# Layer 2: GpSimd's indirect stores, gathers and scatters wait for TensorE's progress

## The chip, the cores and the metric

The kernel is one program on 1 core of one Trainium2 chip. The metric is the device time of one execution in microseconds (us), lower is better.

## What is computed

The input is x, 32 sequences of 128 tokens with 128 channels, and a context of the same shape. Two layers follow each other. Each adds gated cross attention (16 heads of 8 channels) and then a gated mixture of 8 experts. Cut to what matters for the change:

```python
x = x + tanh(g_xattn[0]) * attention0(layernorm(x), ctx)
x = x + tanh(g_ffn[0])   * experts0(layernorm(x))      # one expert of 8 a token, 128 -> 256 -> 128
x = x + tanh(g_xattn[1]) * attention1(layernorm(x), ctx)
x = x + tanh(g_ffn[1])   * experts1(layernorm(x))      # two experts of 8 a token, 128 -> 512 -> 128

# experts1: the two best experts of each token, and their normalised weights
probs = softmax(xt @ gate_w.T); top_w, top_i = top_k(probs, 2)
top_w = top_w / (top_w.sum(-1, keepdims=True) + 1e-9)
out = (take(gelu(xt @ w1 + b1) @ w2 + b2, top_i) * top_w).sum(experts)
```

## The kernel before

**Attention.** The 32 sequences are 16 pairs. A layer's attention is a software pipeline: `pair_slots` runs rows p = -4 .. 16 (here "row" means one pass of that loop, some 9 to 12 us), and in each row every engine does its part for pairs at different stages. TensorE's order inside a row is written out by hand in eight units. A unit has `scores_for_maxima` (L954, four matmuls whose maxima VectorE takes in L1435) and one `scores` (L936), which adds 1 to the semaphore `s_banks` and which ScalarE turns into exponentials in L737. L1097 multiplies them with the values. `s_banks` thus counts TensorE's units; in row p, 8 * a.g - 4 + u is its value when u units of the row are done.

**Experts.** `tile_slots` works on tiles: 39 tiles of 128 tokens in layer 1, 39 tiles of 256 token places in layer 2 (a "turn" is one tile's pass here). In turn i of layer 2 TensorE transposes tile i+1 (L915, adds 1 to `xg_t`), does the first product of tile i (L1229, `h_done`) and the second one of tile i-1 (L1251, `y_done`). ScalarE copies the transposed tile (L872), scales the results of tile i-2 (L896, `y_scaled`) and does the gelus (L885). VectorE copies the expert's weights (L1846), works out where the results go (L1853 to L1861, `META_ROW`) and adds the bias to the result of tile i-1 (L1871, into `YS`, eight buffers deep; `y_kept`). Before the second product of tile i-1 TensorE waits for `y_kept` of tile i-2, since both use bank PA.

**GpSimd's indirect DMAs.** GpSimd writes the descriptors of three kinds of transfers in layer 2, and each instruction moves 128 rows picked by an index:

- gathers (L646): the results of layer 1's experts come back for each pair, two a pair, in rows -4 to 2 by the table `GATHERS`. VectorE adds them in L1411.
- stores (L651, `dispatch`): each batch of 128 tokens goes out twice, once to each of its experts' regions in `dispatched`. Groups of pairs are routed as they come (six groups, `GROUPS`). Groups 0 to 3 are stored in the rows p = 7 to 16; there, all stores of a row but the first (`gated`) already wait for a unit each. Groups 4 and 5 follow in `rest_of_stores`, called ahead of the tile loop and in its pass 1; `g_weight` tells that a group is routed.
- scatters (L696): the results of a tile go to their tokens' places in `returned`, two a tile, as soon as ScalarE has scaled them.

SyncE loads a tile's rows (L526) when the groups it may need have landed (`SCAT`, for tiles from 11 on all six groups), when VectorE has the table of tiles (L525), and three tiles ahead of TensorE (`xg_t`). VectorE may write the buffers of tile i again for tile i+8 when scatter i has landed (`await_results`).

Nothing is scheduled by a planner: the order on every engine is that of the code, and the semaphores do the rest.

Of the kernel before, what the change touches and what calls it, by code (L numbers as in the profile page):

```python
# [54 lines left out]
GATHERS = {-4: (2,), -3: (3, 4), -2: (5, 6), -1: (7, 8), 0: (9, 10, 11), 1: (12, 13), 2: (14, 15)}  # L55
# [127 lines left out]
def program(nc, at, x_in, ctx_in, gates_in, wsq_in, wg_in, vec_in, w0_in, w1_in, const_in,  # L183
# [9 lines left out]
    with ExitStack() as ctx:  # L193
# [203 lines left out]

        LOAD_LATER, COMBINE_LATER, STORE_LATER = 7, 6, 11
        COUNTED = (EARLY_GROUP + 2, NEEDED)

        def await_rows(engine, a):

# [159 lines left out]
        def _(pool):  # L562
# [37 lines left out]
            def attention_slot(layer):  # L600
                def slot(p, pair):
                    n, a, z = pair(4), pair(0), pair(-2)
# [4 lines left out]
                    gated = older[1:] if a else []  # L607
# [15 lines left out]
                        nc.gpsimd.tensor_tensor(out=two(n), in0=two(n), in1=BIAS[:, :].unsqueeze(1).broadcast_to([P, 2, D]),  # L623
                                                op=ALU.add).then_inc(x_bias, 1)
                    if layer == 1:
                        for k in GATHERS[p] if p in GATHERS else ():
                            gather_results(Pair(1, k // 4, k % 4))
                    for unit, (k, b) in zip(range(7 - len(gated), 7), gated):
                        pool.wait_ge(s_banks, 8 * a.g - 4 + unit + 1)
                        dispatch(k, b)  # L630
                    if ahead and not a:
                        for k, b in older[2:]:
# [6 lines left out]
                        deviations(z)  # L639
                return slot  # L640

            def gather_results(g):
                if g.p >= 8:
                    pool.wait_ge(combined, g.p - 7)
                for c in range(2):
                    pool.indirect_dma_start(YG[:, g.p % 8, c, :], None, ys[0][:, :],  # L646
                                            bass.IndirectOffsetOnAxis(ap=SLOT[:, 0, g.b + c:g.b + c + 1], axis=0)).then_inc(YGS[g.p % 8], 16)

            def dispatch(k, b):
                d = next(Group(i) for i in range(len(GROUPS)) if Group(i).b <= b < Group(i).b + Group(i).n)  # L650
                pool.indirect_dma_start(xs[:, :], bass.IndirectOffsetOnAxis(ap=SLOT[:, k, b:b + 1], axis=0),  # L651
                                        N[:, b, :], None).then_inc(SCAT[d.k], 16)
# [12 lines left out]
            def rest_of_stores(k, first, end):  # L665

                d = Group(k)
                pool.wait_ge(g_weight, k + 1)
                for i in range(first, end):
                    dispatch(i % 2, d.b + i // 2)  # L670

            def first_experts():
# [13 lines left out]
            def second_experts():  # L686
                rest_of_stores(4, 0, 3)
                deviations(LAST)
                rest_of_stores(4, 3, 12)
                for i in range(TILES[1]):  # L690
                    a = Tile(1, i)
                    if i == 1:
                        rest_of_stores(5, 0, 8)
                    pool.wait_ge(y_scaled, i + 1)
                    for c in range(2):
                        pool.indirect_dma_start(ys[1][:, :], bass.IndirectOffsetOnAxis(ap=META_ROW[:, a.f, c:c + 1], axis=0),  # L696
                                                YS[:, a.f, c, :], None).then_inc(SC[a.f], 16)

            pair_slots(0, attention_slot(0))
            first_experts()  # L700
            pair_slots(1, attention_slot(1))
            second_experts()


# [200 lines left out]
        def _(pe):  # L905
# [223 lines left out]
            def table_counts(part):  # L1129

                n = COUNTED[part]
                pe.wait_ge(totals, part + 1)
# [131 lines left out]
        def _(dve):  # L1264
# [355 lines left out]
            def table_keys(part):  # L1620
# [5 lines left out]
                comparable, valid, minus_k, region, row, limit, key, places, offset = (ONE[:, k:k + 1] for k in range(9))  # L1626
                n = COUNTED[part]
                count = ROWBASE[:, n - 1:n]
# [23 lines left out]
            def table_values(part):  # L1652


                minus_k, region, row, limit = (ONE[:, k:k + 1] for k in (2, 3, 4, 5))
                n = COUNTED[part]
                count = ROWBASE[:, n - 1:n]
# [287 lines left out]
```

## Time and profile before

| | us |
|---|---|
| median of 3 timed runs | 744.86 |
| the three runs | 745.62, 744.86, 735.52 |
| time of the profiled execution | 743.05 |
| its span in the profile | 741.4 |

The span is that of the instructions; the 1.65 us between it and the execution's time lie around it. In the rows below PE is TensorE, DVE is VectorE, ACT is ScalarE, POOL is GpSimd and SP is SyncE; times count from the span's start. Attention of layer 2 runs from about 330 to 547, its experts from there to the end. "Remote" and "another core or an unknown queue" are the profile's names for a wait whose end it can't put down to an instruction; this kernel has one core. "Issue" is time in which an engine waited for nothing that the profile shows. An indirect DMA's row on POOL is the time in which GpSimd writes its descriptors; the data move after it.

### The profile page before, as it was taken

How to read it: one execution, taken by the hardware profiler on the slowest of the kernel's cores; microseconds unless marked ns; L12 is line 12 of the kernel's file. 1: busy time of each engine (PE TensorE's matmuls, PEld its weight loads, DVE VectorE, ACT ScalarE, POOL GpSimd, SP SyncE). 2: the span in 40 equal slices, each digit the busy share in tenths (PEclk: the TensorE clock that was granted, in tenths of full speed). 3: DMA queues.
4: the chain of work that ended last, by engine and by line, in shares of the span. 5: the costliest groups of instructions: out<-in, count | busy, mean ns of one | idle time of the engine just before them, and what ended most of it. 6: DMA issues, size and time to landing. Idle time of an engine off the chain costs nothing.

```text
span 741.4 us, 17439 instructions
## 1 busy us (share of the span) xinstructions
PE 572.9 (77%) x5771; PEld 464.0 (63%) x5771; DVE 486.7 (66%) x1577; ACT 377.5 (51%) x938; POOL 306.3 (41%) x429
## 2 busy tenths in 40 slices
PE   5889999998811057895888988888676639999991
PEld 4667677775610046785656766666465539999991
DVE  5888889986277944434869998888653524336432
ACT  2267677777422023331346766666443526666661
POOL 5412223311100056637543226464656455455543
PEclk9899999999855559998789999999879969999997
DMA  6243444441010013334445545341022112244523
GB/s 187 79 137 114 140 131 127 133 125 37 15 66 1 0 40 87 88 84 113 134 131 156 166 126 170 110 121 54 32 58 79 56 36 80 72 134 150 156 86 108
DMA packets 99863, 72.58 MB, mean 98 GB/s; under 512 B 13272, under 2 KB 93272, under 8 KB 99752
## 3 DMA queue, kind: packets, MB, share of 16 engines
q1 hardware_dynamic: 88496, 53.64, 24.9%
q0 software_dynamic: 6816, 14.10, 6.5%
q10 hardware_dynamic: 4464, 3.73, 1.7%
q8 instruction: 48, 0.79, 0.5%
q14 instruction: 39, 0.32, 0.1%
HBM read 42.14 MB, written 29.85 MB: 97 GB/s over the span
## 4 chain that ended last, share of the span: by engine, by line
PE 53%; DVE 20%; issue 9%; DMA 6%; POOL 3%; another core or an unknown queue 3%; ACT 2%; SPq 2%; POOLq 0%; DVEq 0%; ACTq 0%
PE bank L1229 11%; PE bank L1251 9%; PE bank L915 7%; DVE MX L1435 7%; PE bank L1097 6%; PE bank L954 6%; PE bank L936 4%; PE bank L1243 3%; DMA QS_N<-MH 3%; DVE PT L1753 2%; POOL dispatched L651 2%; PE bank L920 1%; PE bank L1114 1%; DMA KS<-spread 1%
## 5 line engine op out<-in xcount | busy, mean ns | idle before, releaser
L737 ACT ACTIVATE PT<-bank 128x512 f32<-128x512 f32 x256 | 151.6, 600 | 120.0 <-PE bank L936 97.7
L1435 DVE TENSOR_REDUCE MX<-bank 128x4 f32<-128x512 f32 x256 | 171.8, 680 | 41.8 <-PE bank L954 32.7
L954 PE MATMUL bank<-KS,QS_N 96*128 96x128 f16 x1024 | 104.5, 226 | 23.8 <-DVE MX L1435 10.3
L954 PEld LDWEIGHTS bank<-KS,QS_N 96*128 96x128 f16 x1024 | 74.8, 101 | 53.9 <-issue 25.4
L1229 PE MATMUL bank<-XGT,XT_HL_WR 128*128 128x256 f32 (+1 forms) x468 | 101.3, 354 | 8.7 <-ACT XGT L872 7.1
L936 PE MATMUL bank<-QS_N,KS 98*128 98x512 f16 x256 | 100.8, 398 | 6.0 <-DMA QS_N<-MH 4.1
L696 POOL DMA_INDIRECT returned<-PT,META_ROW x78 | 77.2, 990 | 65.9 <-ACT PT L896 49.7
L1251 PE MATMUL bank<-WALL,HT 128*128 x624 | 78.1, 280 | 22.1 <-DVE PT L1871 15.1
L1251 PEld LDWEIGHTS bank<-WALL,HT 128*128 128x128 f32 x624 | 76.7, 195 | 26.1 <-issue 24.2
L1229 PEld LDWEIGHTS bank<-XGT,XT_HL_WR 128*128 128x128 f32 x468 | 78.4, 195 | 18.3 <-ACT XGT L872 9.2
L651 POOL DMA_INDIRECT dispatched<-N,SLOT x64 | 63.6, 994 | 54.0 <-DVE N L1375 30.2
L1097 PE MATMUL bank<-PT,VA 128*32 128x128 f32 x2048 | 74.7, 288 | 3.5 <-ACT PT L737 3.2
L872 ACT ACTIVATE XGT<-bank 128x128 f32<-128x128 f32 (+1 forms) x78 | 25.8, 331 | 93.4 <-PE bank L915 74.4
L679 POOL DMA_INDIRECT PT<-normed,LIST x39 | 38.3, 983 | 79.2 <-DVE LIST L1821 59.5
L1846 DVE COPY XT_HL_WR<-WALL 128x512 f32 (+1 forms) x78 | 35.0, 449 | 51.3 <-PE bank L1243 24.7
L1871 DVE TENSOR_TENSOR PT<-bank,WALL 128x256 f32<-128x256 f32 x39 | 16.6, 425 | 79.3 <-PE bank L1251 52.1
L1097 PEld LDWEIGHTS bank<-PT,VA 128*32 128x32 f32 x2048 | 55.9, 115 | 20.3 <-issue 13.8
L885 ACT ACTIVATE HT<-bank,XT_HL_WR 128x256 f32<-128x256 f32 x156 | 61.6, 470 | 10.0 <-PE bank L1229 5.9
L590 POOL TENSOR_SCALAR MINUS<-MV_N 128x2 f32<-128x2 f32 x31 | 7.3, 234 | 124.7 <-DVE MV_N L1307 124.1
L646 POOL DMA_INDIRECT HT<-returned,SLOT x32 | 31.4, 980 | 18.7 <-DMA returned<-PT 10.1
L920 PE MATMUL bank<-CONST 128*128 128x128 f32 x192 | 33.7, 323 | 0.0
L920 PEld LDWEIGHTS bank<-CONST 128*128 128x128 f32 x192 | 31.2, 233 | 1.6 <-issue 0.6
(245 smaller groups left out, 1013.6 us busy)
## 6 DMA issues: line engine op xcount, KB each, us to landing
spread<-XT_HL_WR SPq DMA_DIRECT2D x96, 128.0 KB
QS_N<-spread SPq DMA_DIRECT2D x128, 48.0 KB
KS<-spread SPq DMA_DIRECT2D x32, 192.0 KB
PT<-dispatched SPq DMA_DIRECT2D x39, 132.0 KB
WALL<-in_w SPq DMA_DIRECT2D x8, 578.0 KB
CT<-in_ctx SPq DMA_DIRECT2D x32, 128.0 KB
returned<-PT SPq DMA_DIRECT2D x39, 64.0 KB
WALL<-in_w ACTq DMA_DIRECT2D x8, 256.0 KB, 2.8
```

The costliest lines, as they stand in the source:

```text
L651: pool.indirect_dma_start(xs[:, :], bass.IndirectOffsetOnAxis(ap=SLOT[:, k, b:b + 1], axis=0), N[:, b, :], None).then_inc(SCAT[d.k], 16)
L696: pool.indirect_dma_start(ys[1][:, :], bass.IndirectOffsetOnAxis(ap=META_ROW[:, a.f, c:c + 1], axis=0), YS[:, a.f, c, :], None).then_inc(S ...
L737: nc.scalar.activation(PT[:, c, 4 * g:4 * g + 4, :].rearrange("p j q -> p (j q)"), ST[i % 2][:, :], ACT.Exp, scale=SCALE[layer]).then_inc( ...
L885: last = nc.scalar.activation(HT[:, a.u, m, :], bank[2 * a.u + m // 2][:, TILE * (m % 2):TILE * (m % 2) + TILE], ACT.Gelu, bias=WR[:, a.t, ...
L915: return nc.tensor.transpose(to, of, ident[0:n, 0:n])
L920: nc.tensor.matmul(to[:, 0:P], ident, ident, start=True, stop=True)
L936: nc.tensor.matmul(ST[i % 2][:, :].rearrange("p (j q) -> p j q", j=J), KS[0:98, x.r, g, c * P:(c + 1) * P], QS[0:98, x.r, J * g:J * g + J, ...
L954: last = nc.tensor.matmul(MB[i % 2][:, j * P:(j + 1) * P], QS[0:96, m.r, J * g + j, c * P:(c + 1) * P], KS[0:96, m.r, g, c * P:(c + 1) * P ...
L1097: last = nc.tensor.matmul(PA[32 * g:32 * g + 32, 256 * c + P * (j // 2):256 * c + P * (j // 2) + P], VA[:, b.r, c, head(g, j), :], PT[:, c ...
L1229: last = nc.tensor.matmul(bank[2 * a.u + m // 2][:, n * (m % 2):n * (m % 2) + n], WR[:, a.t, m * P:(m + 1) * P], XGT[:, a.u, 0:n], start=T ...
L1251: last = nc.tensor.matmul(PA[:, c * D:(c + 1) * D], HT[:, a.u, m, c * P:(c + 1) * P], WALL[:, bass.ds(r + (W1COLS[1] + m * D), D)], start= ...
L1435: V.tensor_reduce(out=MX[:, m.u, 2 * J * g + c:2 * J * (g + 1):2], in_=MB[i % 2][:, :].rearrange("p (j k) -> p j k", j=J), op=ALU.max, axi ...
```

## The change

Nothing is computed differently, and on TensorE, VectorE, ScalarE and SyncE every instruction stays where it was. On GpSimd the order stays too; what is new are waits ahead of some of the indirect DMAs, in layer 2 alone:

- gathers of rows 0, 1 and 2 (14 instructions; in rows below 0 there is no wait): the first of a row waits for 1 unit of the row, the second for 2, and so on up to 6.
- the stores that already waited for a unit in a row now spread over units 2 to 7, where they waited for the last ones (four of them: units 4, 5, 6, 7 before, 2, 3, 5, 7 now; six rows have such stores).
- the stores of groups 4 and 5: by `STORE_BEHIND`, store 5 of group 4 waits for the transposes of tile 3, store 8 for tile 4, store 11 for tile 5; store 2 of group 5 for tile 7 and store 6 for tile 8.
- the scatters of tiles 1 to 15 wait for the transposes of a later tile as well: tile 8 for scatter 1, 9 for 2, 10 for 3 and 4, 11 for 5, 12 for 6 and 7, 13 for 8, 14 for 9 and 10, 15 for 11, 16 for 12 and 13, 17 for 14, 18 for 15.

```diff
+        STORE_BEHIND = {(4, 5): 3, (4, 8): 4, (4, 11): 5, (5, 2): 7, (5, 6): 8}
...
-                        for k in GATHERS[p] if p in GATHERS else ():
-                            gather_results(Pair(1, k // 4, k % 4))
-                    for unit, (k, b) in zip(range(7 - len(gated), 7), gated):
-                        pool.wait_ge(s_banks, 8 * a.g - 4 + unit + 1)
+                        for i, k in enumerate(GATHERS[p] if p in GATHERS else ()):
+                            gather_results(Pair(1, k // 4, k % 4), 8 * a.g - 4 + 2 * i + 1 if a else None)
+                    for i, (k, b) in enumerate(gated):
+                        pool.wait_ge(s_banks, 8 * a.g - 4 + 2 + 5 * i // max(len(gated) - 1, 1))
                         dispatch(k, b)
...
-            def gather_results(g):
+            def gather_results(g, unit=None):
                 if g.p >= 8:
                     pool.wait_ge(combined, g.p - 7)
                 for c in range(2):
+                    if unit and unit + c > 0:
+                        pool.wait_ge(s_banks, unit + c)
...
                 for i in range(first, end):
+                    if (k, i) in STORE_BEHIND:
+                        pool.wait_ge(xg_t, Tile(1, STORE_BEHIND[k, i]).g + 1)
                     dispatch(i % 2, d.b + i // 2)
...
                     pool.wait_ge(y_scaled, i + 1)
+                    if i in range(1, 16):
+                        pool.wait_ge(xg_t, Tile(1, i + 7 - (i - 1) // 3).g + 1)
```

The order on GpSimd in the first passes of layer 2's tile loop, from scatter 0 on. Before (`dispatched` are the stores of group 5, `returned1` the scatters; in brackets the semaphores that an instruction waits for, and x7 says that the row stands seven times):

```order
L696 DMA returned1<-PT,META_ROW 18176x128
L651 DMA dispatched<-N,SLOT 34816x132 [waits g_weight]
L651 DMA dispatched<-N,SLOT 34816x132 x7
L696 DMA returned1<-PT,META_ROW 18176x128 [waits y_scaled]
L696 DMA returned1<-PT,META_ROW 18176x128
```

And now, with the changed kernel's line numbers, the same place:

```order
L703 DMA returned1<-PT,META_ROW 18176x128
L654 DMA dispatched<-N,SLOT 34816x132 [waits g_weight]
L654 DMA dispatched<-N,SLOT 34816x132
L654 DMA dispatched<-N,SLOT 34816x132 [waits xg_t]
L654 DMA dispatched<-N,SLOT 34816x132 x3
L654 DMA dispatched<-N,SLOT 34816x132 [waits xg_t]
L654 DMA dispatched<-N,SLOT 34816x132
L703 DMA returned1<-PT,META_ROW 18176x128 [waits xg_t,y_scaled]
L703 DMA returned1<-PT,META_ROW 18176x128
```

Nothing moved; the eight stores, which had one wait in front, are cut into 2, 4 and 2, and the scatter behind them has a wait for TensorE too.

The gathers of layer 2's row 0 on GpSimd (`HT` holds the gathered rows), before:

```order
L617 TENSOR_TENSOR RSTD<-VE,EXPO 128x2 [waits pool_own]
L646 DMA HT<-returned,SLOT 128x128 [waits combined]
L646 DMA HT<-returned,SLOT 128x128
L646 DMA HT<-returned,SLOT 128x128 [waits combined]
L646 DMA HT<-returned,SLOT 128x128
L646 DMA HT<-returned,SLOT 128x128 [waits combined]
L646 DMA HT<-returned,SLOT 128x128
```

And now:

```order
L618 TENSOR_TENSOR RSTD<-VE,EXPO 128x2 [waits pool_own]
L649 DMA HT<-returned,SLOT 128x128 [waits s_banks,combined]
L649 DMA HT<-returned,SLOT 128x128 [waits s_banks]
L649 DMA HT<-returned,SLOT 128x128 [waits s_banks,combined]
L649 DMA HT<-returned,SLOT 128x128 [waits s_banks]
L649 DMA HT<-returned,SLOT 128x128 [waits s_banks,combined]
L649 DMA HT<-returned,SLOT 128x128 [waits s_banks]
```

Each of the six has a wait of its own for TensorE's units now; the order is the same.

## Rows read from the trace of the kernel before

**Rows 1.** Line L651: what ended GpSimd's idle time before it, us, times

```profile
  PE bank L936: 9.4, 8
```

**Rows 2.** The chain that ended last, in order of time: start us, us, what

```profile
370.76 2.29 another core or an unknown queue
...
379.50 2.07 another core or an unknown queue
...
588.93 14.94 another core or an unknown queue
...
614.07 1.78 PE bank L1251 x16
...
617.80 1.78 PE bank L1251 x16
...
730.70 2.22 DMA returned<-PT,META_ROW
```

**Rows 3.** Timeline of GpSimd, 557 to 620: start us, us, instruction [idle before <-releaser]

```profile
557.91 1.09 POOL L651 DMA_INDIRECT dispatched<-N,SLOT  x1 [0.17 <-issue]
...
563.33 0.96 POOL L651 DMA_INDIRECT dispatched<-N,SLOT  x1 [0.30 <-issue]
...
570.96 0.95 POOL L696 DMA_INDIRECT returned<-PT,META_ROW  x1 [0.30 <-issue]
581.30 0.96 POOL L651 DMA_INDIRECT dispatched<-N,SLOT  x1 [9.39 <-DVE N L1375]
...
600.28 0.96 POOL L696 DMA_INDIRECT returned<-PT,META_ROW  x1 [0.30 <-issue]
605.43 0.95 POOL L696 DMA_INDIRECT returned<-PT,META_ROW  x1 [4.19 <-ACT PT L896]
...
617.68 0.96 POOL L696 DMA_INDIRECT returned<-PT,META_ROW  x1 [1.05 <-ACT PT L896]
```

**Rows 4.** Timeline of TensorE, 563 to 605

```profile
568.68 2.05 PE L1251 MATMUL bank<-WALL,HT 128*128 x16 [3.35 <-issue]
...
584.56 1.95 PE L1251 MATMUL bank<-WALL,HT 128*128 x16
...
587.49 0.38 PE L915 MATMUL bank<-CONST,PT 128*128 128x128 f32 x2
...
604.67 3.60 PE L1251 MATMUL bank<-WALL,HT 128*128 x16 [15.08 <-DVE PT L1871]
```

**Rows 5.** Timeline of VectorE, 561 to 604

```profile
568.01 0.42 DVE L1871 TENSOR_TENSOR PT<-bank,WALL 128x256 f32<-128x256 f32 x1 [6.40 <-remote]
...
574.02 0.42 DVE L1871 TENSOR_TENSOR PT<-bank,WALL 128x256 f32<-128x256 f32 x1 [4.07 <-remote]
...
604.00 0.42 DVE L1871 TENSOR_TENSOR PT<-bank,WALL 128x256 f32<-128x256 f32 x1 [14.89 <-remote]
```

**Rows 6.** Timeline of ScalarE, the same stretch

```profile
603.97 0.38 ACT L872 ACTIVATE XGT<-bank 128x256 f32<-128x256 f32 x1 [13.30 <-remote]
```

**Rows 7.** DMA queues from 589 to 604: packets, MB, share of 16 engines

```profile
q0 software_dynamic: 352, 0.73, 14.5%
q1 hardware_dynamic: 144, 0.14, 3.6%
```

**Rows 8.** Timeline of GpSimd, gathers of layer 2's rows 0 and 1

```profile
364.51 1.07 POOL L646 DMA_INDIRECT HT<-returned,SLOT  x1 [0.19 <-issue]
...
370.91 0.95 POOL L646 DMA_INDIRECT HT<-returned,SLOT  x1 [0.30 <-issue]
...
375.75 1.08 POOL L646 DMA_INDIRECT HT<-returned,SLOT  x1 [0.18 <-issue]
...
379.63 0.94 POOL L646 DMA_INDIRECT HT<-returned,SLOT  x1 [0.30 <-issue]
```

**Rows 9.** Timeline of ScalarE behind these gathers

```profile
373.11 0.60 ACT L737 ACTIVATE PT<-bank 128x512 f32<-128x512 f32 x1 [2.81 <-remote]
...
381.63 0.60 ACT L737 ACTIVATE PT<-bank 128x512 f32<-128x512 f32 x1 [3.52 <-remote]
```

## The prediction, made before the changed kernel ran

> **What bounds the kernel now.** I read the chain that ended last first. In layer 2's experts it is TensorE alone: from one second product to the next it takes 3.73 us (617.80 - 614.07, [rows 2]), the turns of the last 33 tiles run like that, and GpSimd isn't on that chain until its last scatter. But ahead of these turns the chain has a piece of 14.94 us that belongs to nothing ("another core or an unknown queue", at 588.93), and two more in attention, 2.29 and 2.07 us (370.76 and 379.50, [rows 2]). The question is what these are, since the change touches only GpSimd's indirect DMAs.
>
> The timelines of the four engines answer it. TensorE ran the second product of a tile at 584.56 and the transposes of tile 8 at 587.49 [rows 4]. VectorE needs only the first for its addition L1871, ScalarE only the second for its copy L872. Yet VectorE starts at 604.00 after 14.89 us of idleness, ScalarE at 603.97 after 13.30 [rows 5, 6], within 0.03 us of each other, and TensorE, which needs VectorE's addition, at 604.67 after 15.08 [rows 4]. So TensorE had done the work, but the others didn't learn of it: its semaphore counts were held back. What GpSimd does in that time is a run of 16 indirect DMAs from 581.30 to 601.24 (600.28 + 0.96), 0.3 us apart, eight stores and the scatters of tiles 1 to 4 [rows 3]. The hold ends 2.7 us behind the last.
>
> The same picture stands at every long run. The stores of group 4 and scatter 0 are 11 in a row from 557.91 to 571.9 (570.96 + 0.95, [rows 3]); VectorE waits 6.40 and 4.07 us for "remote" [rows 5], the second time until 2.1 us behind the run, and TensorE is idle for 3.35 us before 568.68 [rows 4]. The six gathers from 364.51 end at 371.86, and ScalarE goes on at 373.11 (1.25 us later); the four from 375.75 end at 380.57, and it goes on at 381.63 (1.06 later) [rows 8, 9]. Where GpSimd pauses after two, as with the scatters from 605.43 on (a wait of 1.05 us ahead of 617.68, [rows 3]), the turns keep 3.73 us. My reading: a run of indirect DMAs can hold back TensorE's counts, mostly until 1 to 2.7 us after the run stops (568.01 came in the middle of one, so not always). What makes it is not in the trace; that they coincide is.
>
> **The change part by part.** Its new waits are on TensorE's counts. While these are held, GpSimd stops at the next wait, and stopping is what ends the hold. The waits thus bound the hold; where no hold exists they are nearly met on arrival, since GpSimd is behind TensorE there. I take 1.25 us as the time from the end of a run to the release.
>
> *Stores of group 4 and scatter 0.* Stores 3 to 11 and two scatters ran in one piece. Now store 8 waits for tile 4. The one ahead of it starts at 563.33 and ends at 564.3 [rows 3]; the release comes at about 565.5, not 568.01: 2.5 us. The second hold (4.07 us) is cut by the wait ahead of store 11, by about 1.6, as three more DMAs still follow that wait. Sum -4.1. Bounds: 0, if holds begin anew at once, and -7.4, TensorE's 3.35 and VectorE's 4.07 us gone.
>
> *Stores of group 5 and scatters 1 to 4.* The idle 15.08 us of TensorE is what is at stake [rows 4]. The run of 16 becomes 2, 4, 4 (two stores and scatter 1) and then twos. The first four take 4 x 1.26 = 5.0 us (spacing from [rows 3]: (600.28 - 581.30) / 15 = 1.26) and with the release 6.3; TensorE can go on for about one turn, 3.73, before it lacks VectorE's addition, so up to 3.2 us remain of that hold allowing 0.6 for the addition and its wait, and 2.2 of the next, which finds GpSimd partly through. 15.1 - 5.4 = 9.7 us gained. Bounds: 0 and -15.1.
>
> *Scatters that share a wait.* 3 with 4, 6 with 7, 9 with 10, 12 with 13: four in a row, 5.0 + 1.25 - 3.73 - 1.4 (the scatters start behind the transposes) = 1.1 us each if each is held; I take half of four: +2.2, bounds 0 and +4.4. All these scatters ran on time before, from 605.43 on.
>
> *Gathers.* In row 1 the second gather waits for unit 2, so the hold of 375.75 to 381.63 should end sooner; in row 0 the first four waits count layer 1's units and are met, only the sixth can stop. 1 us for row 0, 1.5 for row 1, of the 2.29 and 2.07 on the chain [rows 2]: -2.5, bounds 0 and -4.4. The results aren't late: gather 11 of row 0 is added in row 1, behind five of its units.
>
> *Gated stores of groups 0 to 3.* They move by a unit or two to the front, but most find their unit done: TensorE ended only 9.4 us of GpSimd's idle time ahead of the 64 stores, in eight waits [rows 1]. The last one still waits for unit 7. I take 0, bounds -1 and +1.
>
> *What stands behind the waits.* Behind a waiting store are the other stores; tile 11's load needs them all. But it also needs the table that VectorE writes in turn 8, later than store 7 of group 5 (which goes in turn 7), so it hides 2.5 us of stores; without that cover TensorE would wait for the load. Behind scatter 1 stands the reuse of its buffers by tile 9 in VectorE's turn 8. Counted from tile 8's transposes: two stores and two scatters 5.0 us, landing 1.3 (the last scatter of all is issued at 730.70, written by 731.65 and on the chain for 2.22 us, [rows 2]), 6.3 in all; TensorE lacks the result only after 2 turns plus some 1.4 us, 8.9. Slack 2.6 us, so 0.
>
> Sum: 743.05 - 4.1 - 9.7 + 2.2 - 2.5 + 0 = 728.95 us on the profiled execution's own time. The median of the runs lies 1.81 above it, so 730.8; I say **730**.
>
> **Rivals.** *(a) The holds vanish.* Short runs aren't held at all, as in the last 33 turns: 743.05 - 7.4 - 15.1 - 4.4 = 716.2, with the 1.8 us to the median 718, and up to 721 with what stays of row 0. For it: pairs are clean [rows 3]. Against: four gathers in a row were held [rows 8, 9].
>
> *(b) The run is not the cause.* Then the 15 us come back wherever, and the time is 743 to 745. The engines all stand still together, as they would if they lacked instructions. The DMA queues from 589 to 604 show only GpSimd's and the hardware's own packets, and none of the instruction kind [rows 7], which speaks against it; so does that both engines resume as the run ends. In the Trainium skill, page "Runtime: NRT & Kernel Launch", section "Instruction fetch mechanics", instructions are fetched in blocks by DMA of the sequencer's own, and a block that isn't there stalls the engine; by that, waits on GpSimd would change nothing. No packet in [rows 7] agrees. Likewise "SBUF — State Buffer", section "Who interferes with whom", says that a DMA never contends with a compute engine; by that the run couldn't hold TensorE up and the sum would be 743. The trace has 14.89 us of VectorE waiting beside it [rows 5], so I weigh it little.
>
> *(c) Slower.* A hold begins at every new piece. The waits from store 5 of group 4 to scatter 12 name 13 different tiles; at each, both sides stop in turn: GpSimd waits for a held count, and the count waits for GpSimd to be still. At 2.7 us each, the longest release seen, that is 35.1 us against the 15.1 + 7.4 recovered: 743.05 + 12.6 = 755.7, 757 at the median. It decides from 1.7 us a wait on. For it: the release of 568.01 was followed by a second hold within 3 us [rows 5]. Against: the last 33 turns have a pair each and no such stop.
>
> *(d) The waits do little*, since holds last whatever GpSimd does (568.01 ended in mid-run, so some end by another clock): half of the gain, 743.05 - 7 + 1.8 = 738.
>
> **How the numbers follow.** Forecast (724 to 735) 0.51; (a) 0.17; (d) 0.13; (b) 0.12; (c) 0.07. The timed runs of before themselves spread by 10 us, more than any fixed part of the work explains, which fits holds of changing length. The range 719 to 744 leaves out (c), half of (b) and the tip of (a), some 0.17 in all. Two per cent, about what a measurement of this kernel can tell from no change, is 14.9 us: 729.96 is the border, and the forecast lies on it. Faster by over 2%: (a) 0.17 and half of the forecast's case, 0.43. Slower by over 2% needs 759.8, a bad (c): 0.04. Within 2%: the rest, 0.53.
>
> **What would show it.** In the profile after, no piece of over 6 us without an owner between 575 and 605; VectorE's idle time before L1871 put down to "remote" falls from 6.40 + 4.07 + 14.89 = 25.4 us to below 12; GpSimd's stores 2 and 6 of group 5 and scatters 1 to 4 start behind waits that TensorE ended; the turns stay at 3.73 us. Wrong would be: a hold of ten or more us with GpSimd standing still (then (b)); many holds of 1 to 3 us, one for each wait (c); VectorE waiting for a scatter's landing before L1853 or L1855, or SyncE's load of tile 11 ending a wait of TensorE.

## The result, and the profile after

| | before | after |
|---|---|---|
| median of 20 timed runs, us | 743.40 | 737.27 |
| their range, us | 735.52 to 746.95 | 731.59 to 740.75 |
| profiled execution: time, span, us | 743.05, 741.4 | 732.34, 730.7 |

The ratio is 0.9928, 95% interval 0.9905 to 0.9952: faster by 0.7%, some 6 us, and less than two per cent. The time lies inside the range of the prediction, but the gain is less than half of the 14.9 us that stood there (744.86 - 730). The profiled execution flatters the change: it is 10.7 us shorter than that of before, and 7.7 us of this lie ahead of layer 2's first gather (it starts at 323.6 us, before at 331.3), where both programs are the same. This part varies from execution to execution (323.8 to 330.4 us in the other kernels of this study), so below I compare the parts behind it.

In the changed kernel the lines are 7 further down: the second product is L1258, VectorE's addition L1878, the copy of a transposed tile L879, the gelus L892, the scatters L703, the stores L654. The chain of waits, in order of time (start us, us, what), answers to [rows 2]:

```profile
362.42 1.27 another core or an unknown queue
...
370.63 2.16 another core or an unknown queue
...
557.31 3.77 another core or an unknown queue
...
563.17 2.59 another core or an unknown queue
...
593.74 4.38 another core or an unknown queue
...
598.94 2.77 PE bank L1258 x16
...
604.45 2.48 another core or an unknown queue
607.91 3.41 another core or an unknown queue
...
662.28 1.78 PE bank L1258 x16
```

The piece of 14.94 us is gone. In its place stand pieces of up to 4.4 us, among them those of 593.74, 604.45 and 607.91, where the chain of before had TensorE's turns of 3.73 us and nothing else. In attention both pieces are still there, 8 to 9 us earlier, as all of layer 2 is: 2.29 us behind the gathers of row 0 became 1.27, and 2.07 us behind those of row 1 became 2.16. GpSimd's timeline (start us, us, instruction, idle before it and what ended it), 573 to 622, answers to [rows 3]:

```profile
573.44 0.96 POOL L654 DMA_INDIRECT dispatched<-N,SLOT  x1 [3.89 <-DVE N L1382]
...
575.97 0.96 POOL L654 DMA_INDIRECT dispatched<-N,SLOT  x1 [0.30 <-issue]
...
582.64 0.95 POOL L654 DMA_INDIRECT dispatched<-N,SLOT  x1 [1.93 <-remote]
...
589.25 0.95 POOL L703 DMA_INDIRECT returned<-PT,META_ROW  x1 [1.67 <-remote]
...
595.59 0.96 POOL L703 DMA_INDIRECT returned<-PT,META_ROW  x1 [0.30 <-issue]
598.91 0.96 POOL L703 DMA_INDIRECT returned<-PT,META_ROW  x1 [2.36 <-remote]
...
602.63 0.96 POOL L703 DMA_INDIRECT returned<-PT,META_ROW  x1 [1.50 <-PE bank L922]
...
609.05 0.96 POOL L703 DMA_INDIRECT returned<-PT,META_ROW  x1 [0.30 <-issue]
612.34 0.96 POOL L703 DMA_INDIRECT returned<-PT,META_ROW  x1 [2.34 <-remote]
```

The run of 16 is cut, but not into 2, 4, 4 and twos. At 575.97 store 2 found its wait met and went on (0.30 us, "issue"), and so did scatter 1 at 585.16, so the pieces are 6, 4, 6, 2, 6 and 6 DMAs. The six from 589.25 to 596.55 (595.59 + 0.96) are scatters 2, 3 and 4: when the first was let through, tile 10's count came in while it and the next were being written. Each piece of six ends in a wait of GpSimd's own of 1.9 to 2.4 us for a count that TensorE had passed: a small hold. VectorE's timeline in that stretch, to be read beside [rows 5]:

```profile
591.93 0.42 DVE L1878 TENSOR_TENSOR PT<-bank,WALL 128x256 f32<-128x256 f32 x1
...
598.26 0.42 DVE L1878 TENSOR_TENSOR PT<-bank,WALL 128x256 f32<-128x256 f32 x1 [4.39 <-remote]
```

And TensorE's, beside [rows 4]:

```profile
592.61 2.05 PE L1258 MATMUL bank<-WALL,HT 128*128 x16 [0.78 <-DVE PT L1878]
...
598.94 2.05 PE L1258 MATMUL bank<-WALL,HT 128*128 x16 [2.33 <-DVE PT L1878]
...
602.77 1.95 PE L1258 MATMUL bank<-WALL,HT 128*128 x16
```

VectorE waits 4.39 us for "remote" until 598.26, 1.7 us behind the run of six, and TensorE's next second product comes 6.33 us after the last (598.94 - 592.61), not 3.73. Summed over the kernel, VectorE's waits of this kind fell little (the view of waits; us in total, times, longest):

```profile
DVE PT L1878 <- remote: 21.5, 7, 4.4
```

Before, it was 25.4 us in 3 waits; I had said below 12.

**A measure for all kernels.** The start of a second product less that of the one before it, less 3.73 us, is what a turn costs beyond TensorE's own work: its extra time. 39 tiles make 38 gaps. In us:

| gaps | before | after |
|---|---|---|
| 1 to 4 (stores of group 4, scatter 0) | 1.8, 3.9, 3.0, 1.5 | 1.5, 1.3, 1.0, 1.8 |
| 5 to 8 (stores of group 5, scatter 1) | 0.1, 16.4, 1.8, 0 | 0.1, 3.4, 1.0, 1.0 |
| 9 to 16 | 0, all | 2.6, 0.1, 0, 2.9, 0.6, 1.6, 0.1, 1.4 |
| sum of 1 to 8 | 28.5 | 11.1 |
| sum of 9 to 36 | 0.0 | 10.5 |

The change takes 17.4 us out of the first eight turns and puts 10.5 back into the later ones.

Gap 7 of before, 1.8 us, is the hold's as well. The views of windows of both kernels (stretch, its length, busy us of TensorE, its weight loads, VectorE, ScalarE and GpSimd, then the granted clock as a share of full speed), first before, then after:

```profile
604.00:608.50 4.50, 3.83 (x22) 3.82 (x23) 2.88 (x18) 2.49 (x7) 2.16 (x2) 0.56 0.06 21
575.00:604.00 29.00, 22.35 (x152) 19.61 (x151) 14.98 (x78) 14.11 (x41) 17.27 (x19) 1.00 0.24 70
```

After its 15.08 us of idleness TensorE starts again at the lower of its two clock levels (0.50, which is 1.2 GHz, from 604 to 606), and the second product takes 3.60 us [rows 4] where it takes 1.95 at 1.00. In the changed kernel no wait of TensorE there is over 2.33 us, and the granted clock stays at 1.00 from 557 to 714. So a long hold costs more than its idle time, which the prediction didn't count.

So the questions for the chip were: which part does what, what causes the holds, and why do the later turns cost 10 us.

### The profile page after: what moved, and what is told of

The parts are those of the page before. It is cut to its first block, busy times and chain, and to the rows that moved or that the text cites. A ratio compares the mean times of both kernels' runs of the same rounds, so it can differ in the third digit from the quotient of the medians.

```text
span 730.7 us, 17461 instructions
## 1 busy us (share of the span) xinstructions
PE 570.3 (78%) x5771; PEld 458.1 (63%) x5771; DVE 489.4 (67%) x1577; ACT 377.3 (52%) x938; POOL 306.7 (42%) x429
## 3 DMA queue, kind: packets, MB, share of 16 engines
q10 hardware_dynamic: 4464, 3.73, 1.8%
## 4 chain that ended last, share of the span: by engine, by line
PE 52%; DVE 23%; issue 10%; DMA 4%; ACT 3%; another core or an unknown queue 3%; SPq 1%; POOL 1%; DVEq 1%; POOLq 0%; ACTq 0%
PE bank L1236 9%; PE bank L922 7%; PE bank L1258 7%; DVE MX L1442 7%; PE bank L1104 6%; PE bank L961 6%; PE bank L943 5%; PE bank L1250 3%; DVE PT L1760 2%; DMA QS_N<-MH 2%; PE bank L1022 1%; PE bank L1121 1%; PE bank L1024 1%; PE bank L927 1%
## 5 line engine op out<-in xcount | busy, mean ns | idle before, releaser
L703 POOL DMA_INDIRECT returned<-PT,META_ROW x78 | 77.3, 990 | 61.5 <-ACT PT L903 32.3
L1236 PEld LDWEIGHTS bank<-XGT,XT_HL_WR 128*128 128x128 f32 x468 | 79.3, 198 | 14.9 <-ACT XGT L879 6.9
L1258 PE MATMUL bank<-WALL,HT 128*128 x624 | 78.0, 278 | 12.9 <-ACT HT L892 4.7
L1258 PEld LDWEIGHTS bank<-WALL,HT 128*128 128x128 f32 x624 | 74.1, 192 | 21.6 <-issue 20.6
L654 POOL DMA_INDIRECT dispatched<-N,SLOT x64 | 63.5, 993 | 52.1 <-DVE N L1382 23.4
L892 ACT ACTIVATE HT<-bank,XT_HL_WR 128x256 f32<-128x256 f32 x156 | 61.6, 473 | 20.7 <-remote 11.6
L879 ACT ACTIVATE XGT<-bank 128x128 f32<-128x128 f32 (+1 forms) x78 | 25.8, 331 | 73.6 <-PE bank L922 55.9
L1878 DVE TENSOR_TENSOR PT<-bank,WALL 128x256 f32<-128x256 f32 x39 | 16.6, 425 | 68.1 <-PE bank L1258 45.9
L649 POOL DMA_INDIRECT HT<-returned,SLOT x32 | 31.5, 984 | 18.8 <-DMA returned<-PT 10.2
L1250 PE MATMUL bank<-XT_HL_WR,HT 128*128 128x128 f32 x156 | 26.6, 296 | 6.9 <-issue 5.0
L903 ACT ACTIVATE PT<-PT,META_W 128x128 f32<-128x128 f32 x78 | 27.1, 398 | 9.3 <-DVE PT L1878 6.7
```

The costliest lines, as they stand in the source:

```text
L892: last = nc.scalar.activation(HT[:, a.u, m, :], bank[2 * a.u + m // 2][:, TILE * (m % 2):TILE * (m % 2) + TILE], ACT.Gelu, bias=WR[:, a.t, ...
L1236: last = nc.tensor.matmul(bank[2 * a.u + m // 2][:, n * (m % 2):n * (m % 2) + n], WR[:, a.t, m * P:(m + 1) * P], XGT[:, a.u, 0:n], start=T ...
L1250: last = nc.tensor.matmul(bank[6 + a.u][:, 0:D], HT[:, a.u, m, 0:P], WR[:, a.t, w:w + D], start=(m == 0), stop=(m == M - 1))
L1258: last = nc.tensor.matmul(PA[:, c * D:(c + 1) * D], HT[:, a.u, m, c * P:(c + 1) * P], WALL[:, bass.ds(r + (W1COLS[1] + m * D), D)], start= ...
```

## The experiments

Each kernel was timed in five rounds, four at a time beside the same runs of the kernel before; the ratio is to before. First the parts alone.

**Stores alone (e1).** The waits of the scatters and of the rows are taken out again:

```diff
-                    if i in range(1, 16):
-                        pool.wait_ge(xg_t, Tile(1, i + 7 - (i - 1) // 3).g + 1)
```

> The change's waits of the stores of groups 4 and 5 alone; gathers, gated stores and scatters as before. Theory (a run of indirect DMAs without a pause holds TensorE's counts until it stops): the run of 11 is cut as in the changed kernel, 4 to 5 us gained there; the run of 16 begins two stores later and goes on through the scatters of tiles 1 to 6 without a wait, so a hold of some 8 to 12 us stays. About 737 to 741, ratio 0.990 to 0.997. Rival (the waits of the stores are all that counts, since the runs of scatters do no harm): as the changed kernel or better, 0.985 to 0.993.

**Scatters alone (e2).** Only the two lines that e1 takes out are added to the kernel before.

> The change's waits of the scatters of tiles 1 to 15 alone. Theory: the eight stores of group 5 and scatter 1 are still ten in a row, so a hold of 7 to 10 us instead of 15 stays, and behind it GpSimd catches up with holds of 1 to 3 us, 8 to 12 us in all. 741 to 746, ratio 0.997 to 1.003. Rival (the scatters' waits do the work): 0.990 to 0.995.

**Rows alone (e3).** Only the gathers' waits and the spread of the gated stores are added to the kernel before.

> The change's waits in the rows of attention alone (gathers of rows 0 to 2, gated stores spread). The prediction's term: 2.5 us gained, 741, ratio 0.9966. The two profiles differ by 3.9 us up to the first expert product, which would be 0.995. Rival: the difference of the two profiles is chance, and the ratio is 0.999 to 1.001.

**The change with a slower catch-up (e5).** A scatter falls back on its own tile by one tile in six:

```diff
-                    if i in range(1, 16):
-                        pool.wait_ge(xg_t, Tile(1, i + 7 - (i - 1) // 3).g + 1)
+                    if i in range(1, 34):
+                        pool.wait_ge(xg_t, Tile(1, i + 7 - (i - 1) // 6).g + 1)
```

> The whole change, but scatter i waits for tile i+7-(i-1)//6 instead of i+7-(i-1)//3, for tiles 1 to 33: GpSimd catches up by one tile in six turns, not in three. Theory (the loss behind turn 7, 12 us in the changed kernel's profile, is that of runs of four to six scatters while GpSimd catches up): pairs with a pause behind them are clean as in the last turns before, and one four in six turns costs 1 to 2 us, 3 to 6 in all; 728 to 732, ratio 0.980 to 0.986. Rival 1 (each scatter costs what it costs): as the changed kernel, 0.992. Rival 2 (scatters so late make VectorE wait for the buffers of a tile eight later): 0.995 to 1.01, with VectorE's idle time before L1853 or L1855 in the profile.

| | median us | ratio (95%) | extra, gaps 1 to 8 | 9 to 36 |
|---|---|---|---|---|
| e1 stores | 736.11 | 0.9903 (0.9868 to 0.9938) | 22.0 | 3.1 |
| e2 scatters | 739.04 | 0.9948 (0.9921 to 0.9975) | 18.9 | 10.1 |
| e3 rows | 744.98 | 1.005 (1.0015 to 1.0085) | 30.8 | 0.7 |
| e5 slow catch-up | 735.40 | 0.9884 (0.9845 to 0.9922) | 11.3 | 13.4 |

With the stores' waits alone the long hold moves to where the next long run begins, 14 DMAs from 583.81 to 601.62, and gaps 5 to 9 cost 19.0 us together, where before has 18.3. TensorE's timeline of e1:

```profile
588.99 2.05 PE L1256 MATMUL bank<-WALL,HT 128*128 x16 [0.60 <-issue]
...
604.77 3.78 PE L1256 MATMUL bank<-WALL,HT 128*128 x16 [10.38 <-DVE PT L1876]
```

It loses 12.0 (604.77 - 588.99 - 3.73) and 2.6 us in gaps 8 and 9 (the product of 3.78 us behind the hold is again one at a granted clock of 0.50), and the turns behind them are clean, as before. Timed, that gives as much as the whole change, so what the scatters' waits add to the stores' can't be told from nothing by the times: e1 has 0.9868 to 0.9938, f1 below, which has both and no waits in the rows, 0.984 to 0.9925. The scatters' waits alone leave gap 6 at 5.5 us and cost 10.1 later. The rows' waits make the kernel slower by 0.5%, and the slow catch-up spreads its extra time over gaps 13 to 27 without making it less (13.4 against 10.5), so e5 misses its expectation of 0.980 to 0.986.

**Without the rows' waits (f1), gathers alone (f2), gated stores alone (f3).** f1 is the change less what e3 has; f2 and f3 are the halves of e3.

> The change without its waits in the rows of attention: the waits of the stores of groups 4 and 5 and of the scatters. Theory (the parts add up: the rows' waits alone measured 1.005, and they cost the whole change that much): 0.9928 less 0.005 is 0.988, about 733 to 735. Rival (the rows' waits only looked slow, or only cost when the later holds are there too): as the whole change, 0.992 to 0.994.

> Of the change only the gathers' waits for units in rows 0 to 2. The prediction had 2.5 us of gain for it, 0.9966. In the profiles of the change and of the rows alone these waits hardly end any idle time of GpSimd, so they should be without effect: 0.999 to 1.001. Rival (they are what costs in the rows): 1.003 to 1.006.

> Of the change only the spread of the gated stores over units 2 to 7. Theory (spreading them forward joins them to the store or chain ahead and splits the row into two holds in place of one, which costs): 1.003 to 1.007. The prediction had 0. Rival (it is the gathers): 0.999 to 1.001.

f1: 733.73 us, ratio 0.9883 (0.984 to 0.9925), with 13.3 us of extra time in gaps 1 to 8 and 9.5 behind them. f2: 742.39, 1.0008 (0.9977 to 1.0039). f3: 744.91, 1.0031 (0.9998 to 1.0064). The gathers' waits gain nothing, and in f2 both pieces of the chain stand as before, with 2.25 and 2.14 us. GpSimd's timeline of the changed kernel, the gathers of row 1, which were held as before, says why:

```profile
366.88 1.08 POOL L649 DMA_INDIRECT HT<-returned,SLOT  x1 [0.18 <-issue]
368.26 0.95 POOL L649 DMA_INDIRECT HT<-returned,SLOT  x1 [0.30 <-issue]
369.51 0.94 POOL L649 DMA_INDIRECT HT<-returned,SLOT  x1 [0.30 <-issue]
370.76 0.94 POOL L649 DMA_INDIRECT HT<-returned,SLOT  x1 [0.30 <-issue]
```

The four are as close as in [rows 8]; none stopped. They wait for the fifth to the eighth of layer 2's units, and TensorE ran those from 359.92 to 365.93, before the first of the four is written. ScalarE stands idle for 3.88 us until 372.84 behind them, as it did for 3.52 before [rows 9]. In rows 0 and 2 no gather lost time to its wait either. What the spread of the gated stores costs isn't seen in one execution: attention from the first gather to the first second product took 224.2 us before, 228.0 after and 230.0 in f3, but also 218.8 to 227.8 in the eleven others that have the rows of before there. Their mean with those of before and f2 is 225.2, that of the five with the gated stores spread 227.4; some 2 us is what f3's ratio says too. But the two sets overlap (the five go from 222.6 to 230.0), and f3's interval includes 1, so only e3's ratio is clear of 1.

**Pauses of another kind (g1).** This one asks what causes a hold. It is the kernel before, with one new wait (for the end of attention, ahead of the tile loop), and with `memset`s of 96x2048 on GpSimd as pauses between DMAs, into memory that nobody reads any more:

```diff
                 for i in range(first, end):
+                    if (k, i) in ((4, 5), (4, 8), (4, 11), (5, 2), (5, 6)):
+                        pause()
                     dispatch(i % 2, d.b + i // 2)
...
                     pool.wait_ge(y_scaled, i + 1)
+                    if i in range(2, 9):
+                        pause()
```

> The kernel before, with a memset of 96x2048 on a dead buffer (1.8 us of GpSimd, seen at the kernel's start) in the runs of layer 2's experts: ahead of stores 5, 8 and 11 of group 4, stores 2 and 6 of group 5, and the scatters of tiles 2 to 8. It adds 12 memsets to what is done; nothing waits for TensorE. Theory (indirect DMAs back to back hold the counts, and any gap of over 1.3 us between them ends it): the piece of 15 us goes as in the changed kernel, and as GpSimd catches up in pairs with gaps, few holds follow; 729 to 737, ratio 0.982 to 0.992. Rival (GpSimd being busy without rest is what holds the counts, or only waiting for TensorE helps): the hold stays or grows by the memsets' time, 1.00 to 1.02.

Measured: 741.48 us, ratio 0.9981 (0.9944 to 1.0018), which neither the theory nor the rival had; the timelines tell more. GpSimd's timeline at the end of the pauses:

```profile
618.57 1.82 POOL L666 MEMSET QS_N<- 96x2048 f32 x1
620.90 0.96 POOL L704 DMA_INDIRECT returned<-PT,META_ROW  x1 [0.51 <-POOL QS_N L666]
...
637.34 0.96 POOL L704 DMA_INDIRECT returned<-PT,META_ROW  x1 [0.30 <-issue]
642.73 0.95 POOL L704 DMA_INDIRECT returned<-PT,META_ROW  x1 [4.44 <-ACT PT L904]
```

And TensorE's in the same stretch:

```profile
618.13 1.95 PE L1259 MATMUL bank<-WALL,HT 128*128 x16
...
621.86 1.95 PE L1259 MATMUL bank<-WALL,HT 128*128 x16
...
627.42 2.05 PE L1259 MATMUL bank<-WALL,HT 128*128 x16 [1.66 <-issue]
...
641.74 3.78 PE L1259 MATMUL bank<-WALL,HT 128*128 x16 [6.75 <-ACT HT L893]
...
648.48 1.95 PE L1259 MATMUL bank<-WALL,HT 128*128 x16
```

With a pause of 1.8 us after each pair of scatters the turns are 3.73 us (gaps 9 to 14 cost 0.1 us together), though GpSimd is hardly ever idle. The pauses end at 620.4; the fourteen scatters from 620.90 to 638.30 follow without one, and TensorE loses 1.8 + 10.6 + 3.0 us there, where before has clean turns. Gap 6, 16.4 us before, costs 4.8 in turn, and gaps 1 to 8 cost 15.7 together. So a hold is made by the run without a pause: not by a place in the program, not by GpSimd being busy, and a wait for TensorE isn't needed to prevent it. It gains nothing here since the memsets put GpSimd further behind: when TensorE starts tile 14's second product it has begun 17 scatters, 27 before. Those ten are 12.6 us of its time, and gaps 9 to 36 cost 15.6.

**How to pay the debt.** When TensorE starts tile 8's second product (gap 9), GpSimd has begun 7 scatters in the changed kernel and 14 before, and both are even again at the last tile. So the waits leave it 7 scatters in debt, 7 x 1.26 = 8.8 us of its time, while TensorE goes on; in a turn of 3.73 us it has 3.73 - 2.52 = 1.2 us to spare, and that is the pause. Before, it paid them inside the 15 us hold. The remaining kernels pay in other ways. f4 is f1 with e5's rate of one tile in six; h1 is f4 with scatter 1 ahead of group 5's stores; h2 is f1 with no catching up; e4 is the changed kernel again:

```diff
 h1, against f4:
-                    if i == 1:
+                    if i == 2:
                         rest_of_stores(5, 0, 8)
...
-                    if i in range(1, 34):
+                    if i in range(2, 34):
...
 h2, against f1:
-                    if i in range(1, 16):
-                        pool.wait_ge(xg_t, Tile(1, i + 7 - (i - 1) // 3).g + 1)
+                    if i in range(1, TILES[1] - 7):
+                        pool.wait_ge(xg_t, Tile(1, i + 7).g + 1)
```

> Waits of the stores and scatters as in the change, none inside the rows, and scatters fall back on their tiles by one tile in six instead of one in three, up to tile 33. The two runs above gave 0.9884 for the slow catch-up with the rows' waits and 0.9883 for the fast one without them. If the rows' waits cost about 0.3 to 0.5% by themselves (0.5% measured alone) and the slow catch-up saves some 0.4% beside the change, both together give 0.984, about 731. If the two only moved the same microseconds from turn to turn, it stays at 0.988, about 734; and the extra time of the turns behind turn 8 still adds to some 12 us, only spread over more turns.

> As the kernel with the slow catch-up and no waits in rows, but scatter 1 goes ahead of the eight stores of group 5 instead of behind them, so GpSimd enters the catch-up one pair (2.5 us) less behind. If the loss behind turn 8 is GpSimd's debt (DMAs that it owes while TensorE needs its pauses), the sum of the turns' extra time from turn 8 on falls by about 2 us and the ratio is 0.003 below that of the kernel without it. If it is not a debt but a price of every wait, nothing falls. If the stores come too late for the load of tile 11, TensorE has one new wait of some us near turn 9 or 10 that SyncE's load ends.

> No catching up at all: every scatter i from 1 on waits for the transposes of tile i + 7, as far as there are such tiles; the stores' waits stay, the rows have none. GpSimd then issues one pair per turn with a pause, and the seven or eight pairs that it still owes come behind the last tile. If running without a pause is what costs turns 9 to 17 their 11 us, those turns go back to 3.73 us (extra time below 0.3 us each), and the end pays instead: about 16 scatters at 1.26 us, 20 us, of which some 13 lie beside TensorE's last two turns and the closing work, so the last part grows by 7 to 8 us. Net 3 to 4 us below the kernel with the fast catch-up and no rows' waits: about 730, ratio 0.983. If each wait has a price of its own, turns 9 to 33 each show some 0.5 to 1 us and the time is 745 or more.

> The changed kernel again, on the same chip and beside the same runs of the kernel before as the three others. 0.990 to 0.995 as before. It is there to tell whether the versions without waits in the rows beat it.

| | median us | ratio (95%) | extra, gaps 1 to 8 | 9 to 36 |
|---|---|---|---|---|
| f4 one in six, no rows | 727.57 | 0.9891 (0.9852 to 0.9931) | 10.9 | 9.4 |
| h1 and scatter 1 first | 725.10 | 0.9847 (0.9804 to 0.9889) | 9.5 | 8.4 |
| h2 no catch-up | 757.93 | 1.029 (1.0243 to 1.0337) | 9.6 | 30.2 |
| e4 the change again | 729.28 | 0.9893 (0.9853 to 0.9932) | 10.9 | 8.9 |

(Before was 736.02 us beside these four, 742.8 beside the eight above and 741.36 beside the four below. These four and the four below ran on the same chip, so the kernel before alone moves by 5 us from one set of runs to the next; only ratios are compared, and small differences between two sets are not safe even so.) h2 is the telling one. GpSimd's timeline around 600:

```profile
601.37 0.96 POOL L703 DMA_INDIRECT returned<-PT,META_ROW  x1 [1.54 <-PE bank L922]
...
605.07 0.96 POOL L703 DMA_INDIRECT returned<-PT,META_ROW  x1 [1.48 <-PE bank L922]
```

TensorE's from there to the first turn that is not clean:

```profile
601.67 1.95 PE L1258 MATMUL bank<-WALL,HT 128*128 x16
...
605.40 1.95 PE L1258 MATMUL bank<-WALL,HT 128*128 x16
...
646.45 1.95 PE L1258 MATMUL bank<-WALL,HT 128*128 x16
...
661.99 2.75 PE L1258 MATMUL bank<-WALL,HT 128*128 x16
```

Each pair waits for TensorE and the fifteen turns from gap 9 on cost 0.0 us extra each: a wait has no price of its own. But I had overlooked who waits for the late scatters. The chain of h2 has it:

```profile
646.91 2.36 DMA returned<-PT,META_ROW
...
652.79 5.26 DMA PT<-dispatched
...
658.78 3.41 PE bank L1236 x8
```

SyncE's queue has loads of finished results (from `returned`) between the loads of tiles, and each waits for all scatters of its tokens. At seven tiles of lag SyncE waits for them, the tile loads behind it are late, and TensorE has no tile: 11.8, 7.9 and 8.6 us in gaps 24, 30 and 34, 5.2 in gap 38, and from the last second product to the end it takes 4.6 us longer (20.9 against 16.3). The expectation of 730 us was wrong by this.

**The shape of the payment (h4, h5, h6), and h1 again (h7).** h4 is f4 with a wait for each single scatter, three in one turn and two in the next; h5 is the same with scatter 1 first; h6 has three in each turn.

```diff
-                    if i in range(1, 34):
-                        pool.wait_ge(xg_t, Tile(1, i + 7 - (i - 1) // 6).g + 1)
                     for c in range(2):
+                        n = 2 * i - 2 + c
+                        if 0 <= n and i < 30:
+                            pool.wait_ge(xg_t, Tile(1, 8 + 2 * (n // 5) + n % 5 // 3).g + 1)
```

> Catch-up of another shape: stores as in the change, no waits in rows, but each single scatter has its own wait, and GpSimd issues three scatters in one turn and two in the next, instead of four in one turn in six. It owes the same five pairs and is even with TensorE at tile 26. Four scatters take 4 x 1.26 = 5.0 us, more than a turn of 3.73, so a catch-up turn runs into the next pair and makes six in a row; three take 3.8. If what costs the 9 to 10 us is those runs of six and the hold behind them, the turns behind turn 8 lose below 0.3 us each and 3 us in all: about 6 us less than with one tile in six, ratio 0.981. If the debt costs the same however it is paid, the turns' extra time stays at 9 to 10 us, spread over more turns, and the ratio stays at 0.989.

> The same three-two rhythm, with scatter 1 ahead of the stores of group 5. If runs of six are the price: ratio 0.978, the lowest of all. If the debt is: the 0.985 of the kernel with scatter 1 first and one tile in six.

> As the one above with three scatters in every turn until GpSimd is even with TensorE: 3 x 1.26 = 3.8 us against a turn of 3.73, so GpSimd has no pause for some ten turns although each scatter waits for a tile's transposes. If a pause is what ends or prevents a hold, this makes a long run again, with holds of some us every few turns (6 to 12 us in turns 9 to 20, ratio 0.985 to 0.99). If it only counts that no more than three are issued between two waits for TensorE, it is as good as three and two, 0.978.

> The kernel with scatter 1 ahead of group 5's stores and one tile in six again, beside the same runs of the kernel before as the three others: 0.985, as in its first measurement, if that was not chance; 0.989 if it was.

| | median us | ratio (95%) | extra, gaps 1 to 8 | 9 to 36 |
|---|---|---|---|---|
| h4 three, two | 729.81 | 0.9805 (0.9756 to 0.9854) | 10.9 | 7.0 |
| h5 the same, scatter 1 first | 729.95 | 0.9820 (0.9774 to 0.9866) | 10.7 | 8.4 |
| h6 three, three | 729.83 | 0.9835 (0.9786 to 0.9884) | 10.6 | 8.9 |
| h7 is h1 again | 734.14 | 0.9895 (0.9858 to 0.9932) | 9.2 | 11.8 |

The best three differ by nothing that can be measured; by their medians all three stand at 0.984 of before. h1 came out at 0.9847 once and at 0.9895 the second time (h7), so part of its gain was chance; scatter 1 ahead of the stores isn't worth anything that shows, and at tile 8's second product h1 has begun the same 7 scatters as f4. h4's ratio is the one that was expected if runs of six were the whole price, but its extra time is not: 7.0 us in gaps 9 to 36, where that theory had below 3. GpSimd's timeline of h4:

```profile
600.01 0.96 POOL L704 DMA_INDIRECT returned<-PT,META_ROW  x1 [1.66 <-remote]
601.27 0.95 POOL L704 DMA_INDIRECT returned<-PT,META_ROW  x1 [0.30 <-issue]
603.77 0.96 POOL L704 DMA_INDIRECT returned<-PT,META_ROW  x1 [1.54 <-PE bank L923]
605.03 0.95 POOL L704 DMA_INDIRECT returned<-PT,META_ROW  x1 [0.30 <-issue]
606.29 0.96 POOL L704 DMA_INDIRECT returned<-PT,META_ROW  x1 [0.30 <-issue]
608.59 0.96 POOL L704 DMA_INDIRECT returned<-PT,META_ROW  x1 [1.34 <-remote]
...
613.64 0.96 POOL L704 DMA_INDIRECT returned<-PT,META_ROW  x1 [0.30 <-issue]
616.69 0.96 POOL L704 DMA_INDIRECT returned<-PT,META_ROW  x1 [2.09 <-remote]
```

Two, then three, as written; but a two whose wait ends late (608.59) is still being written when the count for the three comes, and five go in a row until 614.60, with a hold behind them. In all kernels that catch up during clean turns, eleven executions, gaps 9 to 36 cost 7.0 to 13.4 us, 9.7 on the mean, near the 8.8 us that GpSimd owes, at one tile in three, one in six, three and two, or three in each turn. Two executions of one program differ by 1.6 (the change and e4) and 3.4 us (h1 and h7), so the lower 7.0 of h4 isn't told apart.

**A version that beats the kernel before, and perhaps the change.** h4 to h6 have intervals below that of the change (0.9805, 0.9820 and 0.9835, the highest bound 0.9884, against 0.9905 to 0.9952). With the change's second measurement, 0.9893 (0.9853 to 0.9932), their intervals touch or overlap. They were not timed beside e4, and e4's median, 729.28 us, is no longer than theirs. So they beat the kernel before for certain (h4 by 1.5 to 2.4%); that they beat the change, by some 1%, is not shown. What they have in common is no wait in the rows and a catch-up in small steps, but f4 and h7 have no wait in the rows either and stand at 0.989.

## Why the prediction was right and wrong

**The mechanism** was right: runs of indirect DMAs hold TensorE's counts back, a pause ends or prevents the hold, and rival (b), that the run isn't the cause, fell: by the change itself (14.94 us gone), by e1, where the hold moved with the run, and above all by g1, which made a hold of 10.6 us at a new place by a new run. In the Trainium skill, page "Runtime: NRT & Kernel Launch", section "Instruction fetch mechanics", an engine stalls for a block of instructions that isn't there; by that, pauses of GpSimd's would change nothing, and g1's brought gap 6 from 16.4 us to 4.8. In the Trainium skill, page "SBUF — State Buffer", section "Who interferes with whom", a DMA never contends with a compute engine; by that there would be no hold, and the runs have it, as counts that come late. Whether a port has any part in that no run here shows. Rival (c), a price on every wait, fell with h2: fifteen turns with a wait each cost 0.0 us. Its sign, several holds of 1 to 3 us, was there, but only in the first eight turns and while GpSimd caught up. Rival (a), the holds vanish, fell with the 11.1 us left in gaps 1 to 8. Rival (d) gave the measured time most nearly, 738, but not by its reason: the waits do most of what they should in the first eight turns. Of the signs of being right, the piece of over 6 us is gone, but VectorE's waits for "remote" are 21.5 us and not below 12, and store 2 and scatter 1 didn't stop.

**Term by term**, in the extra time of the gaps:

| term | forecast | measured |
|---|---|---|
| stores of group 4, scatter 0 | -4.1 | -4.6 (10.2 to 5.6) |
| stores of group 5, scatters 1 to 4 | -9.7 | -12.8 (18.3 to 5.5; of the 18.3, 1.8 lie in gap 7, behind the hold) |
| scatters that share a wait | +2.2 | +10.5, and +8.9 in a second execution |
| gathers | -2.5 | 0 (f2: 1.0008) |
| gated stores | 0 | +2.3 (f3: 1.0031, 0.9998 to 1.0064) |

**The step that failed** is "Scatters that share a wait", with its bound of +4.4: it was mis-sized, +2.2 us forecast and +10.5 measured (+8.9 in the second execution). Two things were wrong in it. I took a shared wait as the only way to four in a row; in fact, once GpSimd is behind, the next count is there when it asks, and a four becomes a six (589.25 to 595.59), with a hold that makes the turn 2.6 us longer. And I wrote that "all these scatters ran on time before, from 605.43 on" without asking what had made them so: the hold itself had stopped TensorE for 15 us while GpSimd issued what it owed. Taking the hold away leaves the debt, 7 scatters or 8.8 us, and paying it in clean turns costs about what it is; only h2, which doesn't pay it there, has those turns clean. That is why 17.4 us gained in eight turns became some 7 to 9 in all.

**The gathers' term** failed because the argument went from the hold to the wait and not from the wait's own count: which unit TensorE has reached as GpSimd comes there. A wait bounds a hold only where it stops GpSimd, and in row 1 none did (366.88 to 371.70). Together with the gated stores, at 0 +- 1 forecast, the rows' waits lose 0.5% (e3, 1.0015 to 1.0085), 1 to 6 us. How, no profile of one execution shows; that stays open.

**The slack** that I had counted for those who wait behind held in the change: no load of tile 11 and no landing of a scatter ended a wait of TensorE there. It is not large: at a lag kept at seven tiles (h2) SyncE's loads of finished results made it the bound.

The chance of 0.53 for "within 2%" had the right case; a range down to 719 leaned too much on the gain.

## What to carry to other kernels

Before a stall is costed as a gain, ask what other engines finish in its shade: an engine with 2.5 us of work in a turn of 3.7 that is given eight more pieces at once will owe them, and removing the stall only makes the debt visible. Pacing decided here how evenly the price is spread, and hardly how high it is; fewer pieces would be the next thing to try, which no run here did. A pacing wait does something only where its count isn't there yet; read from the trace when it is reached, and put none where it is met on arrival.

## What the runs showed of the hardware

- A run of GpSimd's indirect DMAs, 128 rows each and 1.26 us apart, without a pause, makes the counts of TensorE come late at VectorE, ScalarE and GpSimd itself, mostly until 1 to 2.7 us behind the run; some come through in its middle (568.01 before, ScalarE at 596.15 and 601.05 in e1). Six in a row cost TensorE 1.4 to 3.4 us in the changed kernel, 16 in a row 16.4 us and 1.8 more, 30 of them in pairs with a pause of some 1.5 us nothing (h2).
- The pause may be other work of GpSimd: a memset of 1.82 us does as well as a wait (g1).
- A long hold also costs clock. After 15.08 us of idleness (before), 10.38 (e1) and 6.75 behind a wait of 2.42 (g1), TensorE started again at a granted clock of 0.50, and its second product took 3.60, 3.78 and 3.78 us, where it takes 1.95 at 1.00.
- The mechanism behind it is still not in any trace: what is shown is that it goes where the run goes.
